# Attention and experts on one core: fewer unread products between the scores, a token's two choices added on VectorE

## The reference

```
x = x + attention(layernorm(x), ctx, ctx)   # 16 heads of 8, ctx is 120 rows per batch
x = x + experts(layernorm(x))

scores = qh @ kh.T / sqrt(8); probs = softmax(scores); concat(probs @ vh) @ wo.T + bo

scores = softmax(xf @ gate_w.T)             # 8 experts
sel = top_k(scores + expert_bias, 2)        # the 2 choices of each of the 8192 tokens
out = sum over the 2 choices of  h @ w2[e],  h = silu(xe @ w1[e]) * (xe @ w3[e]),  xe = token * its score
```

## Time and profile before

| | us |
|---|---|
| median of three runs (867.53 to 871.38) | 871.06 |
| the profiled execution | 866.23 |
| its span | 864.2 |
| PE busy | 720.2 |
| DVE, ACT, POOL busy | 494.9, 419.3, 437.7 |
| attention on TensorE, from about 20 us to about | 440 |
| experts, from about 504 us to about | 826 |
| adding up, to the end | 864 |

### The profile page before, as it was taken

One profiled execution on the slowest core, in us unless ns is written; L12 is line 12 of the kernel. 1 busy time (PEld: TensorE's weight loads), 2 busy tenths in 40 slices (PEclk: granted clock), 3 DMA queues, 4 the chain that ended last, 5 costly groups with the idle time before them and its releaser, 6 DMA issues.

```text
span 864.2 us, 24903 instructions
## 1 busy us (share of the span) xinstructions
PE 720.2 (83%) x7007; PEld 577.8 (67%) x7008; DVE 494.9 (57%) x1404; ACT 419.3 (49%) x935; POOL 437.7 (51%) x779
## 2 busy tenths in 40 slices
PE   1689999999999999999963359999999999999800
PEld 1356677666777776676642158989999899898800
DVE  2446667675777776777743425555555555554536
ACT  1246677676677776776551024444444444443300
POOL 6311127665667675665566724555555545445510
PEclk9969999998999999999995769999999999999965
DMA  2445455565666656655300112212121222212179
GB/s 57 142 118 144 130 143 157 136 178 164 162 174 162 169 135 159 164 153 157 75 27 32 59 34 58 59 55 58 58 61 52 59 57 55 61 52 58 38 268 315
DMA packets 99774, 94.84 MB, mean 110 GB/s; under 512 B 15015, under 2 KB 89385, under 8 KB 99632
## 3 DMA queue, kind: packets, MB, share of 16 engines
q1 hardware_dynamic: 82832, 72.81, 31.5%
q0 software_dynamic: 8416, 16.86, 5.7%
q10 hardware_dynamic: 8448, 4.20, 1.6%
HBM read 55.00 MB, written 39.26 MB: 109 GB/s over the span
## 4 chain that ended last, share of the span: by engine, by line
PE 59%; DMA 12%; issue 9%; SPq 6%; DVE 6%; POOL 5%; ACT 2%; DVEq 0%; POOLq 0%; ACTq 0%
PE m_b L1190 7%; PE score_b L999 7%; PE u_b L1039 6%; PE score_b L957 4%; PE turned_b L1021 4%; PE score_b L198 3%; POOL expert_rows L440 3%; DMA head_rows<-qk 2%; SPq L236 2%; DVE nm L530 2%; PE m_a L1180 2%; PE turned_b L200 2%; PE turned_b L199 2%; PE score_b L200 2%; PE turned_b L198 2%
## 5 line engine op out<-in xcount | busy, mean ns | idle before, releaser
L471 POOL DMA_INDIRECT expert_results<-v,where x135 | 132.9, 984 | 156.8 <-DMA expert_results<-v,where 133.7
L530 DVE TENSOR_REDUCE nm<-score_b 128x8 f32<-128x960 f32 x128 | 148.2, 1158 | 96.4 <-PE score_b L999 92.8
L440 POOL DMA_INDIRECT expert_rows<-rows,places x128 | 128.9, 1007 | 71.0 <-POOL rows L434 49.7
L842 ACT ACTIVATE pT<-turned_b 120x1024 f32<-120x1024 f32 x128 | 130.9, 1023 | 61.2 <-PE turned_b L1021 46.4
L921 ACT ACTIVATE v<-score_b 128x352 f32<-128x352 f32 x135 | 62.7, 464 | 116.0 <-PE turned_b L200 114.9
L1190 PE MATMUL m_b<-w_s,v 128*128 (+1 forms) x810 | 115.7, 279 | 0.6 <-ACT v L926 0.6
L1190 PEld LDWEIGHTS m_b<-w_s,v 128*128 128x128 f32 (+1 forms) x810 | 100.9, 191 | 4.2 <-issue 0.8
L999 PEld LDWEIGHTS score_b<-ks,qs 63*128 63x128 f32 x1024 | 68.8, 192 | 37.2 <-issue 37.2
L769 DVE COPY v<-m_a 128x384 f32<-128x384 f32 x67 | 37.4, 558 | 86.4 <-PE m_a L1180 78.7
L999 PE MATMUL score_b<-ks,qs 63*128 63x120 f32 x1024 | 86.6, 290 | 0.0
L1039 PE MATMUL u_b<-pT,v 120*32 120x128 f32 x2048 | 84.8, 285 | 0.3 <-ACT pT L842 0.2
(11 more groups left out here) (140 smaller groups left out, 1498.8 us busy)
## 6 DMA issues: line engine op xcount, KB each, us to landing
head_rows<-qk SPq DMA_DIRECT2D x32, 496.0 KB
qs<-head_rows SPq DMA_DIRECT2D x192, 64.0 KB
ks<-head_rows SPq DMA_DIRECT2D x96, 120.0 KB
v<-expert_rows SPq DMA_DIRECT2D x135, 64.5 KB, 1.8
v<-expert_results SPq DMA_DIRECT2D x16, 512.0 KB, 5.6
x_s<-in_x SPq DMA_DIRECT2D x32, 128.0 KB, 2.8
out<-pT ACTq DMA_DIRECT2D x16, 256.0 KB, 5.9
c_s<-in_ctx_in SPq DMA_DIRECT2D x32, 120.0 KB
```

Source lines behind the costliest of these rows:

```text
L440: eng.indirect_dma_start(xs_dram, bass.IndirectOffsetOnAxis(ap=places[:, n % 2, u, k:k + 1], axis=0), rows[:, h, k, :], None).then_inc(sca ...
L471: eng.indirect_dma_start(y_dram, bass.IndirectOffsetOnAxis(ap=where[:, q:q + 1], axis=0), y_s[:, q, :], None, bounds_check=2 * T - 1, oob_ ...
L530: eng.tensor_reduce(nm[:, p % 2, :].rearrange("p (a h n u) -> p a h n u", a=2, h=2, u=2)[:, :, h, :, u], score_b[:, :, 0:4 * K].rearrange( ...
L842: eng.activation(pT[0:K, g % 2 * 1024:g % 2 * 1024 + 1024].rearrange("k (a t) -> k a t", a=2), turned_b[0:K, :, :], ACT.Exp).then_inc(c.ex ...
```

## The change

- `scores(g)` issues its unread product only for g under 24. The 104 products of halves 24 to 127 are gone. With the first goes nothing else: the wait for the maxima stays, now on the first of the eight products.
- A new step on VectorE, `all_picked(n)`, adds the two one-hot rows of each token into `picked` (128 x 32). It stands right behind `one_hot(n)` and takes over the wait on the ranks of group n-2 (`c.pos`).
- `ranks(n)` multiplies `picked` and so has five products where it had ten. It waits for `picked` instead of `chosen`.
- `picked` has the fifth row of zeros that `chosen` had; the memset at the start clears `picked`, half the size.

```diff
--- before.py
+++ after.py
@@ -104,7 +104,7 @@
         lmax, ex, esum, rsum = sb("lmax", [P, 4]), sb("ex", [P, 4, E]), sb("esum", [P, 4]), sb("rsum", [P, 4])
         prb, biased = sb("prb", [P, 4, E]), sb("biased", [P, 4, E])
         top, topi = sb("top", [P, 4, 8]), sb("topi", [P, 4, 8], U32)
-        chosen = sb("chosen", [P, 2, 5, 2, E], BF16)
+        chosen, picked = sb("chosen", [P, 2, 4, 2, E], BF16), sb("picked", [P, 2, 5, E], BF16)
         gate_w, gates = sb("gate_w", [P, 4, 2, E]), sb("gates", [P, 2, 4, 2])
         row_of = sb("row_of", [P, 2, 5, E])
         place_w, places = sb("place_w", [P, 4, 2, E]), sb("places", [P, 2, 4, 2], I32)
@@ -150,7 +150,7 @@
         piece_in = [sem(f"piece_in{n}") for n in range(2)]
         ATTENTION = ("stats1 var1 eps1 mean1 rstd1 shift1 xn xbo T T_e qk qh ql kh kl v v_e S max mT nm_e ST exp PV "
                      "U back rden on onT onT_e O x2 stats2 var2 eps2 mean2 rstd2 shift2 xn2 xn2T xn2T_e logits "
-                     "lmax lsub ex esum rsum prb biased top topi chosen gate_w gates pos row_of place_w places "
+                     "lmax lsub ex esum rsum prb biased top topi chosen picked gate_w gates pos row_of place_w places "
                      "rows placed").split()
         c = namedtuple("Attention", ATTENTION)(*[sem("a_" + n) for n in ATTENTION])
         x_in, c_in = [sem(f"x_in{n}") for n in range(3)], [sem(f"c_in{n}") for n in range(3)]
@@ -382,7 +382,7 @@
             const(eng.iota(place_of[:, :, :], [[2, B], [1, 2]], base=0, channel_multiplier=2 * B))
             const(eng.iota(tvec[:, :], [[1, NT]], base=0, channel_multiplier=0,
                            allow_small_or_imprecise_dtypes=True))
-            const(eng.memset(chosen[:, :, :, :, :], 0.0))
+            const(eng.memset(picked[:, :, :, :], 0.0))
             const(eng.memset(ks[:, :, :, :].bitcast(F32), 1.0))
             assert made[0] == N_CONSTS
             eng.memset(padding[:, 0:D], 0.0).then_inc(pad_rows, 1)
@@ -614,12 +614,18 @@
 
             def one_hot(n):
                 eng.wait_ge(c.topi, 4 * n + 4)
-                if due(n - 1): eng.wait_ge(c.pos, n - 1)
                 if due(n - 1): eng.wait_ge(c.place_w, n - 1)
                 eng.tensor_tensor(
                     chosen[:, n % 2, 0:4, :, :],
                     iota_e[:, :].unsqueeze(1).unsqueeze(1).broadcast_to((P, 4, 2, E)),
                     topi[:, :, 0:2].unsqueeze(3).broadcast_to((P, 4, 2, E)), ALU.is_equal).then_inc(c.chosen, 1)
+
+            def all_picked(n):
+
+                eng.wait_ge(c.chosen, n + 1)
+                if due(n - 1): eng.wait_ge(c.pos, n - 1)
+                two = chosen[:, n % 2, :, :, :]
+                eng.tensor_tensor(picked[:, n % 2, 0:4, :], two[:, :, 0, :], two[:, :, 1, :], ALU.add).then_inc(c.picked, 1)
 
             def gate_parts(n):
                 eng.wait_ge(c.chosen, n + 1)
@@ -698,6 +704,7 @@
                 at(best_index, 4 * n - 5, B)
                 at(stats1, 4 * n + 17, B)
                 at(one_hot, n - 2, QUADS)
+                at(all_picked, n - 2, QUADS)
                 at(maxima, 8 * n + 14, HALVES)
                 at(low_q, 2 * n + 5, PAIRS)
                 at(var1, 4 * n + 15, B)
@@ -991,7 +998,8 @@
                     eng.wait_ge(stacked_q, STACK_Q * (p + 1))
                     eng.wait_ge(stacked_k, STACK_K * (p + 1))
                 if due(g): eng.wait_ge(c.max, g)
-                keep_clock_up(16 if g == 0 else 1, score_b[:, 0, :])
+                if g < 24:
+                    keep_clock_up(16 if g == 0 else 1, score_b[:, 0, :])
                 for n in range(4):
                     s, e = 2 * h + n // 2, n % 2
                     for a in range(2):
@@ -1070,16 +1078,13 @@
 
             def ranks(n):
 
-                eng.wait_ge(c.chosen, n + 1)
+                eng.wait_ge(c.picked, n + 1)
                 eng.wait_ge(c.on, min(2 * n + 5, PAIRS))
-                picked = chosen[:, n % 2, :, :, :]
-                for k in range(2):
-                    eng.matmul(m_b[:, 4 * E:9 * E], before[:, :], picked[:, :, k, :], start=(k == 0), stop=False)
+                eng.matmul(m_b[:, 4 * E:9 * E], before[:, :], picked[:, n % 2, :, :], start=True, stop=False)
                 for b in range(4):
-                    for k in range(2):
-                        ins = eng.matmul(m_b[:, (5 + b) * E:9 * E], ones[:, :],
-                                         picked[:, b:b + 1, k, :].broadcast_to((P, 4 - b, E)),
-                                         start=False, stop=(b == 3 and k == 1))
+                    ins = eng.matmul(m_b[:, (5 + b) * E:9 * E], ones[:, :],
+                                     picked[:, n % 2, b:b + 1, :].broadcast_to((P, 4 - b, E)),
+                                     start=False, stop=(b == 3))
                 ins.then_inc(c.pos, 1)
```

## The result

The changed kernel took 889.03, 888.05, 896.82 and 888.76 us, median 888.89. The kernel before, with one more run on the same occasion, has a median of 869.29 us. The ratio is 1.025, with a 95% interval of 1.018 to 1.033. A ratio with an interval leaves out the executions that took over 1.5% more than the fastest of the same kernel; here these mostly show a lower granted clock too, which is what this change is about, so the table of the experiments also has the medians and clocks of all executions. The forecast was 859 us and its range ended at 870, so it was wrong, in sign too. The profiled execution took 889.03 us (span 887.0), 22.8 us more than that of before.

The account below looks back on a forecast made before the run. PE was taken to bound attention, with SP becoming the bound after the change; stretches summed to 11.0 us, less 1.0 for the clock, so mean 869.05 less 10 gave 859 us, forecast range 854 to 863, full range 846 to 870.

Parts of the forecast that it names:

- The clock: TensorE in attention: perhaps one more fall of the clock from longer boundary waits, 1.0 us off the gain, between 0 and 12.
- The mechanism: Rival, attention: without dense products the clock is at half after each of 13 boundaries; 10 us slower, 879; chance 0.13.
- its point of decision: Attention: the clock rival decides the outcome from some five falls more than the few of before, each costing 2.3 us.
- the 5 us of the earlier trace: Attention, 210 to 215 us: one 5 us slice with the clock at 0.53, priced at some 2.3 us of PE's work.
- the experts stage as proof: Experts stage: no unread product, 105 of PE's 301 us transposes, clock 0.99; so attention's clock should hold where PE is full.
- The rule of the Trainium skill: TensorE: the full clock doesn't engage for transposes; by it attention would lose its clock with the dense products gone.
- The products' cost on the path: Attention: the 104 products hold 20.2 us of the chain; removal gives 1.9 us a round, 1.5 after 0.4 goes back.
- SP as the bound: Attention until about 385 us: SP's list and landings limit a round to 23.2 us, giving 1.0 us a round.
- The boundary: Each round's boundary: PE waits 0.8 us for the read-back instead of 0.38, then the exponential; 0.4 us a round goes back.
- Ranks and addition at nothing: Ranks and VectorE's addition, costed at nothing because covered by waits; up to 2 us gain or 2 us loss without cover.
- The end by POOL: Attention's end: POOL's scatters wait for group 12's places, then run unbroken, so what those places gain the program gains.

Follow-up runs that it names:

- e3: Changed kernel with the unread product kept also at each round's boundary (g % 8 == 7), 13 of the 104 back; ratio 1.021 to the kernel before.
- e4: Changed kernel plus three unread products ahead of each round's first turned scores, inside the stand, and one each before halves 125 to 127; ratio 0.991 to before.
- f2: Changed kernel with three unread products inside each round's stand and one each before halves 125 to 127, repeated on another chip; ratio 0.999 to before.
- e6: Changed kernel with three unread products in the middle of each round (g % 8 == 2) and one each before halves 125 to 127; ratio 1.012 to before.
- f3: Changed kernel with three unread products mid-round and one each before halves 125 to 127, run again beside the changed kernel on one chip; ratio 1.019 to before.
- e1: Changed kernel with the unread product kept before all 128 halves, so only the addition and five rank products are new; ratio 0.997 to before.
- e7: Changed kernel with all unread products kept, plus three ahead of each round's first turned scores from half 24 on; ratio 1.000 to before.
- g1: Changed kernel with all unread products kept, plus four into the unused `turned_b` ahead of the maxima wait in halves 1 to 6; ratio 0.994 to before.
- g4: The changed kernel run a third time, unaltered, on a chip where the kernel before took 888 to 890 us; ratio 1.001 to before.
- f1: The changed kernel run again, unaltered, on a chip where the kernel before took 888 to 890 us; ratio 0.996 to before.

## Why the prediction was wrong, step by step

- **The step that failed is "The clock": "there may be one such fall more ... I take 1.0 us off, between 0 and 12".** Measured between 100 and 432 us are six more falls and 61 us more of half clock; over the 104 halves it is 76 us more, an estimated 36.5 us of path. The mechanism stood among the rivals with 0.13, its price (10 us slower, 879) half of what came, and its point of decision, five more falls, was passed by one.
- Two misreadings led there. I priced falls at the 5 us of the earlier trace rows. The products that ended such a stretch soon in before were those that I took away: before, a fall lasted 3.4 to 6.8 us; after, up to 20.5. And I took the experts stage as proof that the clock holds without the products. It shows only that the clock holds where PE seldom stands: in those 322 us two stands were over 1 us, where in attention without the products PE stood that long at nine of 13 boundaries. e3, and e4 and f2 against e6 and f3, show that the inside of the stand is the place where filling helps. A stand alone is not all of it, for the longer of the two in the experts stage left the clock up:

```profile
781.13 0.33 PE L1163 MATMUL m_c<-ident,v 128*128 128x128 f32 x1 [1.78 <-DMA v<-expert_rows]
```

- The rule of the Trainium skill that I weighed (TensorE: Matmul & The Clock Gate, section "Part 4: PE-mode transpose") pointed to the right outcome. Whether transposes have a part in it isn't shown: no run here changed one, and in the experts stage, with 105 us of them, the clock was 0.99.
- **The products' cost on the path was right**: 1.9 us a round less 0.4 given back at the boundary was forecast; rounds at full clock fell by 1.5 to 1.8 us, and the sum of the loss leaves 21.5 us for them where the chain had 20.2.
- **SP as the bound was wrong.** A round of 23.2 us was its price; the rounds at full clock were 22.4 to 22.7. The 8.63 us of the earlier trace rows had `ks` issues in them at 2.83 us that take 1.92 when nothing blocks them.
- **The boundary was right in kind**: between 107 and 435 us PE's waits on `qs<-maxima` rose from 8.3 to 14.3 us, and the wait for the exponential stands in the timeline. It was taken as a loss of 0.4 us; it was the place where the clock fell.
- **Ranks and addition at nothing: right** (e1). **The end by POOL: right**, 20.45 us of delay went through to the end nearly unchanged.

## What to carry to other kernels

An instruction whose result nobody reads may still be doing work: price the clock before its removal, by the stands of TensorE in the trace, and take its length on the path as the upper end of the gain only. Filling instructions belong inside a wait, ahead of the semaphore and into a buffer that is free there; behind the wait (e3) or in the middle of the round (e6, f3) they cost path and held less. A stage in which TensorE seldom stands says little about the clock of one in which it often does.

## What was not expected of the hardware

The chips differ. On the three where the kernel before took 888 to 890 us, from about 140 us on, ScalarE or VectorE stood, mostly for 1.4 to 2.8 us, about once a round before an instruction, and the profile names a releaser outside the core (`remote`), which no trace of the other chips has. From e7's timeline of ScalarE:

```profile
170.65 1.02 ACT L849 ACTIVATE pT<-turned_b 120x1024 f32<-120x1024 f32 x1 [2.64 <-remote]
```

There a product-free round at full clock is 24.8 us (f2) and not 22.5, and the changed kernel is at 0.996 and 1.001. Its clock falls there too: 0.884 and 0.885 over all executions, where the kernel before has 0.916 and 0.915. So the lost clock is seen on every chip, the lost time only where these waits are missing. With them a product costs less (a round at full clock is 25.4 to 25.6 us in g1, with all of them, and 25.0 to 25.3 in g4, with none) and half clock less too: f1's round with 20.5 us of it takes 33.2 us, 0.41 us for each. What the waits are stays open, and so does how these sums close: the kernel before has no profile on those chips. The start is left to chance too: with the same instructions, 14 to 38 us of half clock were seen before 100 us in fifteen profiles, and none at all in the three with the early stands filled.
